# Stage 2 without a break between pairs of heads, and the first mixture's bias added block by block

## The chip, the cores and the metric

The kernel runs on one core of one Trainium2 chip, and the metric is device time in microseconds of one execution. PE is TensorE (its weight loads are PEld), DVE is VectorE, ACT is ScalarE, POOL is GpSimd, SP is SyncE, which here only issues transfers. Engines run their own instruction streams and wait for each other on semaphores.

## What is computed

A model of two layers over x of shape (4, 512, 128), in fp32: first a differential attention with 8 heads, beside a small attention over the batch with a mixture of 8 experts; then four layers of a selective scan with a second mixture. The change is in the first layer. What matters of the reference, cut:

```python
# attention: per head, two halves of q and k (8 columns each), gated by tanh of their difference
# first mixture, on the normed y of shape (2048, 128): each token goes to its argmax expert
idx = jnp.argmax(xf @ Wg.T, axis=-1)
for e in range(8):
    m = (idx == e)[:, None]
    h = jax.nn.relu(xf @ W1[e] + b1[e])
    out = out + m * (h @ W2[e] + b2[e])
# then layernorm of (y + out), a silu gate on the attention's output, and x + the product
```

## The kernel before

`build_stages` (line 48) writes six stages one after the other, each a block in which every engine has its own stream; a barrier of all engines stands between two stages. Tokens are 2048 = 16 tiles of 128. Stages 4 to 6 (line 1189 on: the second mixture, the scans, the output) are not touched.

**Stage 1** (lines 96 to 581) projects, makes q and k as sums of three bf16 parts, and does the small attention. SP stores the parts to `qk_dram` (line 181) and waits for them (line 182). The last work of the stage is the choice of each token's expert on DVE (`first_max`, lines 36 to 43, the last from 106.08 to 106.37 us), which gives `mask0`.

**Stage 2** (lines 588 to 980) has two jobs that share the engines.

The attention goes by steps. A head has 16 steps (4 batches b of 4 key blocks), a pair of heads 32; four steps with the same b are a unit, so a pair has 8 units. Per step PE makes one product into `bank_d` (`difference`, line 784) and two into `bank_l` (`scores`, lines 789 and 790); ACT makes the gate `gt` by tanh (line 877); DVE adds gate and scores into `tt` (lines 967 and 968); ACT takes exp into `ex` (line 883). In the next unit PE multiplies with the values into `bank_pv` (`weigh`, line 822, two halves), ACT copies that to `pvs` (`keep`, line 888), PE turns it back (`turn`, line 830), and DVE sums it into `ybig` (`settle`, line 957). Buffers are 2 banks of each kind and rings of 4 (`RING`). A loop over q, the pairs, is a hardware loop on every engine; at the end of each pass all of the pair's work is drained (lines 857 to 860, 912, 979).

The operands of `difference` and `scores` are the stacks `kst` and `qst` of two heads, [112, 2048] bf16, loaded by `load_head` (line 646) in 12 transfers per head of 32, 64 or 96 KB. At the start ACT loads its table (line 864, 1.28 us), the stacks are cleared (line 708 on POOL, 920 on DVE, two of 0.91 us) and the two first heads loaded, half of the first by ACT (line 870). Later heads are loaded by SP: the pair's next first head in the middle of the pair (line 687), its second at the end (line 696).

The mixture goes by blocks. DVE works out each token's row (lines 924 to 950, with three products on PE, lines 769 to 771, in between); then POOL scatters the 16 tiles into `yx_dram`, sorted by expert (line 735), in 24 blocks of 128 rows (`BLOCKS`; an expert starts a new block), after SP has written zeros there (line 671). Per block: SP loads its rows (`load_block`, line 674), PE turns them (`turn_block`, 796), ACT copies (`keep_in`, 892), PE makes the hidden layer (`hidden`, 802), DVE adds b1 and bounds at 0 (975), PE multiplies with W2 (`block_out`, 808), ACT copies (`keep_out`, 897), SP stores to `yo_dram` (691) and loads the rows two blocks on. POOL gathers a block's weights by indirect transfer (`gather_weights`, 721 to 727) when the block two before is done (`s_dn`). A pair works 6 blocks, in its units 2 to 7; units 0 and 1 have none. PE, ACT and DVE have a fixed order of all this by step, written out by hand (lines 837 to 856, 901 to 911, 961 to 978), and SP and POOL have one queue each:

```python
681 def turn(q, more):
682     for k in range(PER):
683         if k == 2 and more:
685             sp.wait_ge(s_L, step(q, 16))
687             load_head(sp, q * 2 + 2, 0)
689         sp.wait_ge(s_ek, blk(q, k + 1))
691         sp.dma_start(yo_dram[...], eo[k % 2][:, :])...
692         load_block(q * PER + (k + AHEAD), k % 2)
693     if more:
694         sp.wait_ge(s_L, step(q, 32))
696         load_head(sp, q * 2 + 3, 1)
```

**Stage 3** (lines 984 to 1183) norms the attention's output, and POOL gathers the expert outputs back (16 indirect transfers, line 1030), followed on POOL by the factors of two layernorms (`scale_and_offset`, lines 1033 to 1039). The bias b2 is added here: POOL clears `b2blk` (1026), SP fills its diagonal blocks by 16 transfers (1021), PE turns `mask0` (1088) and multiplies (1092, 16 products), and DVE adds the result (1130, 4 times).

## Time and profile before

| | us |
|---|---|
| median of 3 runs (1530.0 to 1530.98) | 1530.02 |
| the profiled execution | 1532.95 |
| its span, first to last instruction | 1530.7 |
| stage 1, to the first instruction of stage 2 | 107.9 |
| stage 2 | 107.9 to 421.7 |
| stage 3 | 421.7 to 475.96 |
| stages 4 to 6 | to 1530.7 |

Busy over the span: PE 82%, DVE 75%, ACT 68%, POOL 63%. A line of the timeline reads: start in us from the start of the span, length in us (a group's, where instructions follow each other, with the count at the end), engine, line, operation, what is written and read; in brackets the time for which the engine had been idle before it and who ended that. In the rows of stages, the clock is the mean granted clock of TensorE (1.00 is 2.4 GHz, 0.50 is 1.2 GHz), and the DMA share is that of the core's 16 DMA engines.

### The profile page before, as it was taken

What the parts mean: (1) busy time and instruction counts of PE and PEld (TensorE: products, weight loads), DVE (VectorE), ACT (ScalarE), POOL (GpSimd) and SP (SyncE); (2) the same over time, 40 slices, a digit from 0 to 9 for tenths busy, and PEclk for the clock granted to TensorE, in tenths of its full rate; (3) what the DMA queues carried; (4) which work ended last, traced back from release to release, by engine and by line L of the source; (5) the groups of instructions that cost most, each with busy time, mean ns of one, the idle gap of its engine ahead of it and who ended that gap; (6) DMA issues with size and microseconds to landing.
All of it is one profiled execution on the core that took longest, in us unless ns stands there. A gap on an engine that the chain in (4) does not pass through costs nothing. (4 is left out here: it accounts for less than half of the span.)

```text
span 1530.7 us, 21758 instructions
## 1 busy us (share of the span) xinstructions
PE 1255.4 (82%) x6427; PEld 620.1 (41%) x6427; DVE 1146.2 (75%) x1605; ACT 1045.8 (68%) x1804; POOL 965.2 (63%) x918
## 2 busy tenths in 40 slices
PE   6454689898836999977798998999899998999884
PEld 3341334343323547633343444444444444444331
DVE  7754468677786321238899999999999999999985
ACT  4323579788834122347588899888898889888871
POOL 5642311010185540058799898988998899989893
PEclk9775789899965999989899999999999999999988
DMA  2112232122214402330342344224341434234301
GB/s 59 42 46 98 89 97 84 65 89 72 86 30 160 132 21 66 114 84 24 83 104 71 77 95 97 71 71 108 85 98 55 99 87 106 59 73 95 93 8 55
DMA packets 84321, 120.47 MB, mean 79 GB/s; under 512 B 17410, under 2 KB 43256, under 8 KB 83848
## 3 DMA queue, kind: packets, MB, share of 16 engines
q1 hardware_dynamic: 77294, 100.60, 25.0%
q0 software_dynamic: 6816, 18.42, 4.0%
q8 instruction: 40, 0.66, 0.2%
q14 instruction: 49, 0.40, 0.1%
q10 hardware_dynamic: 122, 0.39, 0.1%
HBM read 96.15 MB, written 24.77 MB: 79 GB/s over the span
## 5 line engine op out<-in xcount | busy, mean ns | idle before, releaser
L2168 DVE TENSOR_TENSOR_SCAN hs<-decay,dbx 128x512 f32<-128x512 f32 x512 | 591.6, 1204 | 44.0 <-ACT decay L2050 20.4
L1746 POOL TENSOR_TENSOR hcm<-hs,Cc 128x1024 f32<-128x1024 f32 x192 | 452.9, 2367 | 24.6 <-DVE hs L2168 16.4
L2050 ACT ACTIVATE decay<-dtr,a_cur 128x512 f32<-128x512 f32 x512 | 350.7, 710 | 2.2 <-DVE hs L2168 1.9
L1870 PEld LDWEIGHTS dbx<-ident_sb,scaled 128*128 128x128 f32 x1536 | 178.5, 143 | 284.2 <-issue 126.7
L1870 PE MATMUL dbx<-ident_sb,scaled 128*128 128x128 f32 x1536 | 245.2, 284 | 52.8 <-POOL scaled L1729 27.3
L2028 ACT ACTIVATE scaled<-duT,BT 128x256 f32<-128x256 f32 x506 | 224.6, 496 | 27.4 <-PE dbx L1870 26.8
L1739 POOL TENSOR_TENSOR hck<-hs,Cc 128x512 f32<-128x512 f32 x128 | 163.3, 1276 | 54.5 <-DVE hs L2168 50.6
L1867 PE MATMUL dbx<-du,spread_sb 128*128 128x512 f32 x256 | 146.6, 656 | 12.5 <-DVE hs L2168 12.5
L883 ACT ACTIVATE ex<-tt 128x1024 f32<-128x1024 f32 x128 | 136.9, 1070 | 4.4 <-DVE tt L968 3.7
L1797 PE MATMUL slots<-XT,w_tap 128*128 128x512 f32 (+1 forms) x240 | 124.4, 606 | 3.8 <-PEq L1242 3.8
L1729 POOL TENSOR_SCALAR scaled<-duT,BT 128x256 f32<-128x256 f32 x256 | 118.3, 480 | 0.0
L967 DVE TENSOR_TENSOR tt<-bank_l,gt 128x512 f32<-128x512 f32 x128 | 87.5, 683 | 38.3 <-PE bank_l L790 34.6
L723 POOL CAST weight_rows<-w_row 128x1 uint32 (+1 forms) x26 | 4.8, 186 | 167.5 <-PE bank_e L808 167.5
L877 ACT ACTIVATE gt<-bank_d,dgh 128x512 f32<-128x512 f32 x128 | 89.1, 699 | 29.9 <-PE bank_d L784 29.9
L1887 PE MATMUL y_bank<-hcm,fold_sb 128*32 128x512 f32 x768 | 104.4, 616 | 4.2 <-POOL hcm L1746 4.2
L2158 DVE TENSOR_TENSOR dbx<-dbx,Bb 128x512 f32<-128x512 f32 x128 | 88.0, 688 | 23.5 <-PE dbx L1867 23.4
L968 DVE SCALAR_TENSOR_TENSOR tt<-bank_l,gt 128x512 f32<-128x512 f32 x128 | 87.0, 679 | 0.0
L1867 PEld LDWEIGHTS dbx<-du,spread_sb 128*128 128x128 f32 x256 | 43.9, 199 | 92.3 <-DVE hs L2168 46.8
L822 PE MATMUL bank_pv<-ex,v_head 128*32 128x512 f32 x512 | 74.8, 665 | 2.6 <-DVE ybig L957 2.6
L784 PE MATMUL bank_d<-q_stack,k_stack 112*128 112x512 bf16 x128 | 54.4, 430 | 13.4 <-DMA k_stack<-qk_parts 9.0
L1715 POOL MEMSET w_dt<- 41x256 f32 x1 | 0.3, 305 | 100.3 <-POOLq L1242 100.3
L1523 DVE TENSOR_TENSOR hid<-sil,u_bank 128x320 f32<-128x320 f32 x32 | 15.6, 487 | 62.3 <-ACT sil L1430 62.3
(331 smaller groups left out, 2026.5 us busy)
## 6 DMA issues: line engine op xcount, KB each, us to landing
dtr<-dt_turn SPq DMA_DIRECT2D x60, 512.0 KB, 7.7
Cc<-bc_turn SPq DMA_DIRECT2D x256, 64.0 KB, 2.1
dt_turn<-dt SPq DMA_DIRECT2D x15, 512.0 KB, 2.8
Bb<-bc_turn SPq DMA_DIRECT2D x64, 64.0 KB, 2.0
conv_row<-in_conv_row SPq DMA_DIRECT2D x4, 512.0 KB, 5.8
w_rg<-in_w_rg SPq DMA_DIRECT2D x8, 256.0 KB, 2.7
w_ru<-in_w_ru SPq DMA_DIRECT2D x8, 256.0 KB, 3.1
w_rd<-in_w_rd SPq DMA_DIRECT2D x8, 256.0 KB, 3.8
```

Source lines behind the costliest of these rows:

```text
L877: nc.scalar.activation(gt[:, st % RING, :], bank_d[st % 2][:, :], ACT.Tanh, scale=dgh[:, st // 16:st // 16 + 1]).then_inc(s_G, 1)
L883: nc.scalar.activation(ex[:, (st // 4) % 2, st % 4, :, :], tt[:, st % RING, :, :], ACT.Exp).then_inc(s_E, 1)
L1729: nc.gpsimd.tensor_scalar(scaled[:, (n + 1) % 2, kk, :, j, :], duT[:, n % 2, kk, :].rearrange("p (g c) -> p g c", c=32), BT[:, n % 2, kk, ...
L1739: nc.gpsimd.tensor_tensor(hck[:, g % KR, :], hs[:, p % HR, :], Cc[:, 3 + b % 2, :], ALU.mult).then_inc(s_hc, 1)
L1746: nc.gpsimd.tensor_tensor(hcm[:, (m - 1) % MR:m % MR + 1, :], hs[:, q % HR:p % HR + 1:p - q, :], Cc[:, k:k + 1, :].broadcast_to([P, 2, 512 ...
L1797: last = mm(dst[h][:, d:512], w_tap[:, 3 - d, P * h:P * h + P], XT[:, n % 4, 0:512 - d], start=(d == 0), stop=(d == 3))
L1867: mm(dbx[bank_of[p]][:, :], spread[:, g % 4, :], du[:, b % 2, g // 4, :], start=True, stop=True).then_inc(s_bx, 1)
L1870: last = nc.tensor.transpose(dbx[bank_of[p]][:, P * kk:P * kk + P], scaled[:, (b + k) % 2, kk, g, :, :].rearrange("p j c -> p (j c)"), ide ...
L1887: last = mm(y_bank[h][32 * q:32 * q + 32, :], fold[:, :], src, start=False, stop=((k, h) in ((DIRECT - 1, 0), (DIRECT, 1))), tile_position ...
L2028: nc.scalar.activation(scaled[:, (n + k) % 2, kk, :, j, :], duT[:, n % 2, kk, :].rearrange("p (g c) -> p g c", c=32), ACT.Copy, scale=BT[: ...
L2050: nc.scalar.activation(dec[:, p % DR, :], dtr[:, b % 2, g, :], ACT.Exp, scale=a_cur[:, 4 * g + k:4 * g + k + 1]).then_inc(s_dec, 1)
L2168: nc.vector.tensor_tensor_scan(hs[:, p % HR, :], dec[:, p % DR, :], dbx[bank_of[p]][:, :], 0.0, ALU.mult, ALU.add).then_inc(s_sc, 1)
```

## The change

1. The stacks of two heads live in the memory of `XT` and `GATE`, which stages 1 and 2 do not use otherwise. POOL clears the rows that no load writes, in stage 1, and SP loads heads 0 and 1 at the end of stage 1, behind the wait for the stored parts, and waits for them. ACT loads nothing any more.
2. The loop over pairs is one stream of steps: pair "-1" is written out, then a hardware loop of two, then the last pair. There is no drain between pairs; the last steps of a pair and the first of the next follow each other like any others.
3. `PER` is 8: the first pair has no blocks, each of the other three has eight, one in each unit. `BLOCKS` is 24 as before.
4. The working out of the rows (`route`) stands between the steps of the first pair: steps 0 to 4 and 8 to 13 on DVE, its products on PE after step 6. The scatter waits for the first ten steps' result, the gather of weights for the last.
5. SP loads the next heads in the first pair too, and at k = 4 (`PER // 2`) in place of k = 2.
6. b2 of a block's expert is gathered by POOL into `b2[i]` (an indirect transfer of 64 KB ahead of that of the weights, which now wait for `s_ek` in place of `s_dn`); `keep_out` is a DVE addition of `bank_e` and `b2`. What stage 3 did for b2 goes.

```diff
-            BLOCKS = 4 * (-(-(NT + NE - 1) // 4))
+            BLOCKS = 3 * (-(-(NT + NE - 1) // 3))
+            stacks = [tile[:, :, :].rearrange("p a b -> p (a b)").bitcast(bf16) for tile in (XT, GATE)]
+            qst = [stack[0:112, 0:T] for stack in stacks]
+            kst = [stack[0:112, T:2 * T] for stack in stacks]
...
                         sp.wait_ge(s_qkst, 16 * 6 * B)
+                        sp.wait_ge(s_z, 4)
+                        for i in range(2):
+                            load_head(sp, i, i, s_hl)
+                        sp.wait_ge(s_hl, 16 * 2 * LOADS)
...
+                        for stack in (qst[0], kst[0], qst[1], kst[1]):
+                            nc.gpsimd.memset(stack[32:64, :], 0.0).then_inc(s_z, 1)
...
-                        sp.wait_ge(s_z, 4)
-                        load_head(sp, 0, 0, (0,))
-                        load_head(sp, 1, 1)
                         sp.wait_ge(s_zz, 1)
...
+                        def next_head(q, i):
+                            sp.wait_ge(s_L, step(q, 16 * i + 16))
+                            sp.wait_ge(s_zz, 1)
+                            load_head(sp, q * 2 + (4 + i), i, s_ld[i])
+
+                        next_head(-1, 0)
                         sp.wait_ge(s_scat, 16 * NT)
                         for i in range(AHEAD):
                             load_block(i, i)
+                        next_head(-1, 1)
 
                         def turn(q, more):
                             for k in range(PER):
-                                if k == 2 and more:
-                                    sp.wait_ge(s_L, step(q, 16))
-                                    load_head(sp, q * 2 + 2, 0)
+                                if k == PER // 2 and more:
+                                    next_head(q, 0)
                                 sp.wait_ge(s_ek, blk(q, k + 1))
                                 sp.dma_start(yo_dram[bass.ds((q * PER + k) * P, P), :], eo[k % 2][:, :]).then_inc(s_es[k % 2], 16)
                                 load_block(q * PER + (k + AHEAD), k % 2)
                             if more:
-                                sp.wait_ge(s_L, step(q, 32))
-                                load_head(sp, q * 2 + 3, 1)
+                                next_head(q, 1)
-                        with sp.Fori(0, 3) as q:
+                        with sp.Fori(0, 2) as q:
                             turn(q, True)
-                        turn(3, False)
+                        turn(2, False)
...
                         def gather_weights(q, j, i, n):
-                            nc.gpsimd.tensor_copy(at_w[i][:, :], w_row[:, bass.ds(j, 1)]).then_inc(s_cur, 1)
+                            nc.gpsimd.tensor_copy(at_w[i][:, :], w_row[:, bass.ds(j, 1)])
+                            nc.gpsimd.tensor_copy(at_b[i][:, :], e_row[:, bass.ds(j, 1)]).then_inc(s_cur, 1)
                             pool.wait_ge(s_cur, blk(q, n + 1))
+                            nc.gpsimd.indirect_dma_start(b2[i][:, :], None, A["b2"], ...).then_inc(s_wl[i], 16)
                             nc.gpsimd.indirect_dma_start(weights[i][:, :], None, A["w_expert"], ...).then_inc(s_wl[i], 16)
...
                         pool.wait_ge(s_rows, 1)
...
+                        pool.wait_ge(s_rows, 2)
                         for i in range(AHEAD):
                             gather_weights(0, i, i, i)
+                        next_head(-1, 0)
+                        next_head(-1, 1)
...
-                                pool.wait_ge(s_dn, blk(q, k + 1))
+                                pool.wait_ge(s_ek, blk(q, k + 1))
                                 gather_weights(q, q * PER + (k + AHEAD), k % 2, k + AHEAD)
...
+                        def pair_of_heads(q, first=False, final=False):
                             for st in range(STEPS):
                                 u, mb = st // 4, st % 4
+                                if not (final and st >= STEPS - 2):
+                                    difference(q, st + 2, first)
+                                if not (final and st >= STEPS - 1):
+                                    scores(q, st + 1, first)
+                                if first and st == 6:
+                                    rank_tokens()
+                                if mb == 0 and not (first and u < 2):
                                     turn(q, u - 2)
+                                if mb == 0 and not first:
+                                    turn_block(q, u)
...
-                            turn(q, UNITS - 2)
-                            weigh(q, UNITS - 1, 0)
-                            weigh(q, UNITS - 1, 1)
-                            turn(q, UNITS - 1)
...
+                        def keep_out(q, k):
+                            dve.wait_ge(s_dn, blk(q, k + 1))
+                            dve.wait_ge(s_es[k % 2], loaded(q, k))
+                            TT(eo[k % 2][:, :], bank_e[:, 0, :], b2[k % 2][:, :], ALU.add).then_inc(s_ek, 1)
...
+                        def pair_of_heads(q, first=False):
+                            for st in range(STEPS):
+                                u, mb = st // 4, st % 4
+                                sums(q, st)
+                                if mb == 1 and not first:
+                                    relu(q, u)
+                                if mb == 3 and not first:
+                                    keep_out(q, u)
+                                if mb == 0 and not (first and u < 2):
+                                    settle(q, u - 2)
+                                if first:
+                                    route(st)
+
+                        pair_of_heads(-1, first=True)
+                        with dve.Fori(0, 2) as q:
+                            pair_of_heads(q)
+                        pair_of_heads(2)
+                        settle(2, UNITS - 2)
+                        settle(2, UNITS - 1)
...
-                        nc.gpsimd.memset(b2blk[:, :, :], 0.0).then_inc(s_z0, 1)
...
-                            link(TT(part(z, b), part(z, b), bank[4 + b][:, :, :], ALU.add))
```

## Rows read from the trace of the kernel before

**Rows 1.** Stages: us; busy (count) of PE, PEld, DVE, ACT, POOL; clock, DMA, GB/s
```profile
107.90:128.30 20.40, 3.14 (x11) 1.78 (x11) 10.23 (x26) 2.26 (x3) 7.23 (x12) 0.50 0.34 125
128.30:219.80 91.50, 62.37 (x346) 25.70 (x349) 49.19 (x95) 55.02 (x82) 26.11 (x34) 0.76 0.26 82
...
353.80:421.70 67.90, 59.28 (x374) 24.79 (x367) 49.88 (x97) 56.97 (x86) 7.71 (x15) 0.95 0.24 75
421.70:470.30 48.60, 14.11 (x89) 12.21 (x89) 43.24 (x104) 20.40 (x40) 39.58 (x47) 0.65 0.09 23
```

**Rows 2.** Timeline of PE: its three waits for a transfer
```profile
126.58 1.03 PE L784 MATMUL bank_d<-q_stack,k_stack 112*128 112x512 bf16 x2 [8.96 <-DMA k_stack<-qk_parts]
...
164.96 0.45 PE L796 MATMUL bank_e<-ident_sb,block_in 128*128 128x128 f32 x1 [23.39 <-DMA block_in<-block_rows]
...
201.55 0.47 PE L796 MATMUL bank_e<-ident_sb,block_in 128*128 128x128 f32 x1 [2.59 <-DMA block_in<-block_rows]
```

**Rows 3.** Timeline of PE: marks of one unit with a block
```profile
190.85 0.66 PE L830 MATMUL bank_pv<-ident_sb,pvs 128*128 128x128 f32 x4
...
192.20 1.16 PE L802 MATMUL bank_e<-block_inT,expert_weights 128*128 128x128 f32 x8
193.29 1.06 PE L822 MATMUL bank_pv<-ex,v_head 128*32 128x512 f32 x8
...
198.30 0.66 PE L830 MATMUL bank_pv<-ident_sb,pvs 128*128 128x128 f32 x4
```

**Rows 4.** Timeline of ACT: marks of one unit
```profile
209.80 0.60 ACT L888 ACTIVATE pvs<-bank_pv 128x512 f32<-128x512 f32 x1 [0.80 <-PE bank_pv L822]
210.29 0.27 ACT L897 ACTIVATE block_out<-bank_e 128x128 f32<-128x128 f32 x1
210.45 0.69 ACT L877 ACTIVATE gt<-bank_d,dgh 128x512 f32<-128x512 f32 x1
...
211.96 0.29 ACT L892 ACTIVATE block_inT<-bank_e 128x128 f32<-128x128 f32 x1
```

**Rows 5.** Timeline of DVE: first and last sums of pairs, last settle
```profile
128.31 0.69 DVE L967 TENSOR_TENSOR tt<-bank_l,gt 128x512 f32<-128x512 f32 x1 [6.94 <-PE bank_l L790]
...
224.10 0.68 DVE L968 SCALAR_TENSOR_TENSOR tt<-bank_l,gt 128x512 f32<-128x512 f32 x1
...
284.06 0.68 DVE L968 SCALAR_TENSOR_TENSOR tt<-bank_l,gt 128x512 f32<-128x512 f32 x1
...
291.81 0.68 DVE L968 SCALAR_TENSOR_TENSOR tt<-bank_l,gt 128x512 f32<-128x512 f32 x1
...
358.05 0.68 DVE L968 SCALAR_TENSOR_TENSOR tt<-bank_l,gt 128x512 f32<-128x512 f32 x1
...
412.58 0.68 DVE L968 SCALAR_TENSOR_TENSOR tt<-bank_l,gt 128x512 f32<-128x512 f32 x1
...
418.57 0.44 DVE L957 TENSOR_REDUCE ybig<-bank_pv 128x272 f32 x1 [3.50 <-PE bank_pv L830]
```

**Rows 6.** Timeline of SP's issues
```profile
84.43 1.44 SPq L181 DMA_DIRECT2D qk_parts<-part_k  x3
...
194.13 0.35 SPq L674 DMA_DIRECT2D block_in<-block_rows  x1
```

**Rows 7.** Transfer rate while one head loads; columns as in rows 1
```profile
221.00:232.30 11.30, 8.25 (x34) 2.08 (x34) 8.91 (x15) 9.80 (x14) 0.52 (x2) 0.79 0.20 72
```

**Rows 8.** Timeline of POOL: a wait in stage 1, scatter's end, stage 3
```profile
14.04 4.95 POOL L370 TENSOR_TENSOR ACC<-XN,b_mo 128x512 f32<-128x512 f32 x4 [11.89 <-DVE XN L280]
...
160.55 0.98 POOL L735 DMA_INDIRECT block_rows<-Y,row_u  x1 [0.31 <-issue]
...
421.68 1.80 POOL L1026 MEMSET b2blk<- 128x2048 f32 x1 [7.42 <-POOLq L645]
...
424.32 4.83 POOL L1030 DMA_INDIRECT ACC<-block_outs,row_u  x1 [0.80 <-POOL neghalf L1027]
```

**Rows 9.** Tile expert_weights: its gathers, issue to landing
```profile
DMA to landing us min/median/max: 4.4/4.7/8.1
```

More of the change, by code:

```diff
@@ new lines, in keep, with keep_in, pair_of_heads @@
+                        def keep(q, u):
+                            act.wait_ge(s_pvd, unit(q, u + 1))
+                            act.wait_ge(s_pvt, unit(q, u))
+                            nc.scalar.activation(pvs[:, :], bank_pv[:, :], ACT.Copy).then_inc(s_pvs, 1)
+                        def keep_in(q, k):
+                            act.wait_ge(s_xt, blk(q, k + 1))
+                            nc.scalar.activation(xbT[:, :], bank_e[:, 0, :], ACT.Copy).then_inc(s_xk, 1)
+                        def pair_of_heads(q, first=False, final=False):
+                            for st in range(STEPS):
+                                u, mb = st // 4, st % 4
+                                if not (final and st == STEPS - 1):
+                                    gate(q, st + 1)
+                                if not (first and st == 0):
+                                    exps(q, st - 1)
+                                if mb == 3 and not (first and u == 0):
+                                    keep(q, u - 1)
+                                if mb == 0 and not first:
+                                    keep_in(q, u)
@@ L915, in _ @@
+                        gate(-1, 0)
+                        pair_of_heads(-1, first=True)
+                        with act.Fori(0, 2) as q:
+                            pair_of_heads(q)
+                        pair_of_heads(2, final=True)
+                        exps(2, STEPS - 1)
+                        keep(2, UNITS - 1)
                     @block.vector
```

356 lines of the change are left out of this document (158 added, 198 removed).

## The prediction

> **What bounds the kernel now.** The profiled execution took 1532.95 us, its span is 1530.7 us, and the median of the three runs is 1530.02 us. I work out a difference against the profiled execution and take it off the median, since the 2.9 us between them is nothing that the change touches. A change of 0.2% is 3.1 us, about what a measurement of this kernel can tell from no change.
>
> I read the stages first. Stages 4 to 6 begin at 475.96 us and are untouched, so only three stretches count [rows 1]: the opening of stage 2 (107.9 to 128.3 us, DVE busy 10.2 of 20.4), its four pairs of heads (128.3 to 421.7), and stage 3 (421.7 to about 470). The first pair takes 91.5 us and the last 67.9 [rows 1], for the same work. The timeline of PE says why [rows 2]: PE waits 8.96 us for the stacks of q and k before the first product, 23.39 us for the first block's rows in pair 0 (scattered only by then), and 2.59 us for a block's rows at 201.55 us.
>
> Inside a pair two rates matter. A unit of four steps with an expert block is PE's: from one L830 to the next is 7.45 us [rows 3], back to back. The block's `hidden` takes 1.09 us of it (192.20 to 193.29), `block_out` as much, so a unit without a block is 5.27 us of PE at 2.4 GHz. On ACT a step is 1.51 us and the copy of pvs adds 0.49 [rows 4]: 4 x 1.51 + 0.49 = 6.5 us. So a unit without a block is ACT's. At the end of a pair all drains: the last L968 of pair 1 is at 284.06, the first of pair 2 at 291.81, 7.75 us where a step is 1.9 [rows 5].
>
> **The change, part by part.**
>
> *Stacks loaded in stage 1.* SP's last store of stage 1 ends its issue at 85.87 [rows 6]; two more for landing, then 24 loads of 1.57 MB together. One head (786 KB) moves at 72 GB/s [rows 7], so 11 us; two are 22, plus 2 until the first bytes. 88 + 24 gives 112, and as these loads share with nothing better than in that row I take 114 (bounds 112 and 118, the latter at 55 GB/s). Stage 1 else ends at 106.4, so the waiting SP now holds the barrier: 114 + 1.5 = 115.5 for the first instructions of stage 2 (1.5 is the distance 106.4 to 107.9 now). The four memsets of 32 partitions on POOL lie in its wait of 11.89 us that ends at 14.04 [rows 8], and cost nothing. In stage 2 ACT still loads its table (1.28) and runs one gate; the first L967 stands at 117.6, where it is 128.31 now [rows 5]. That is 10.7 us gained; next late is SP, no longer PE.
>
> The row shows 72 GB/s at a DMA share of 0.20 [rows 7]. The Trainium skill ("DMA: Bandwidth & Descriptors", Specifications) gives about 358 GB/s as a core's limit to HBM. By that figure 1.57 MB would take an estimated 4.4 us, stage 1 would end with its own work and the kernel at 1483. The row decides.
>
> *Pair 0 without blocks, with the routing between its steps.* The 26 us at the first block go altogether (23.39 on PE [rows 2]): scatter and gathers now lie under pair 0. Eight ACT units of 6.5 us are 52. PE runs at 1.2 GHz when the stage opens (clock 0.50 [rows 1]); I add 3 us for that. The routing's 8.4 us of DVE (10.23 less the two memsets of stacks, 0.91 each [rows 1]) come on steps in which DVE has 1.2 us of work out of 1.5 to 1.9: I take 5 of the 8.4 as seen. Pair 0 is 60 us; bounds 53 and 71.
>
> Is the first block there in time? Rows are known after step 10, some 23 us into the pair (141); 16 scatters at 1.29 (0.98 + 0.31 [rows 8]) and landing give 164; the loads stand behind head 2's, 168; weights by 170. Pair 1 starts at 178: 8 us to spare.
>
> *Pairs 1 to 3, each with eight blocks and no drain.* Pairs 1 and 2 take 8 x 7.45 = 59.6 each. The last takes what it takes now from its first sums to the last settle, 419.0 - 357.4 = 61.6 [rows 5], plus 3 because its first two units become 14.9; now they are 54.5 less 23 steps of 1.86, 11.7 [rows 3, 5]. The b2 gather on POOL, 24 more, and a cast each, are hidden: POOL is busy 7.7 of 67.9 us [rows 1]. The gather of weights is now asked for after `keep_out` and stands behind that of b2: some 2.6 us later. A block's weights are wanted 14.9 us less about 4.3 after that point, 10.6; needed are 1.3 of casts, 1.3 for b2 and 4.7 for the landing, 7.3, and 10.7 where the landing takes 8.1 [rows 9]. So they just hold. `keep_out` moves from ACT to DVE, which has room (49.9 of 67.9 [rows 1]); it no longer waits behind the copy of pvs, 0.5 us [rows 4].
>
> *Head loads on SP, in the middle of pairs and now between them too.* This is what gives back. Today the load of block 4's rows is issued at 194.13 [rows 6], behind a head's twelve loads, and lands 7.4 us later, at 201.5: PE's wait of 2.59 [rows 2], and a slow clock after it. Its price is the difference of pair 1 and pair 3 from first to last L968: 59.96 - 54.53 = 5.4 us [rows 5]. It falls three times now. With blocks in every unit the same collision comes after the load at k = 4 (pairs 1 and 2) and after the load at a pair's end (pairs 2 and 3), four times; at pair 1's start SP is free three us earlier and I count 0.5. Less the 0.5 of the earlier `keep_out`, 4 x 4.9 + 0.5 = 20.1 us (bounds 0 and 28).
>
> *Stage 3.* The memset of b2blk (1.80), the 16 loads, 16 products and four additions go. The chain there is POOL's, busy 39.6 of 48.6 us [rows 1]: after that memset the gathers, from 424.32 [rows 8], then the factors. It starts 1.8 us earlier. The additions lie beside POOL's work. 1.8 us (bounds 1 and 5.5: the first gather's 4.83 may turn to 1.0).
>
> **Sum.** 117.6 + 60 + 119.2 + 64.6 + 20.1 = 381.5 for the last settle, 419.0 now: 37.5 less. With 1.8 of stage 3, 39.3. 1530.0 - 39.3 = 1490.7; I say 1491 (the profiled execution would be 1493.7).
>
> **Rivals.**
> *Half clock in pair 0.* PE with gaps may keep 1.2 GHz. In the stretch [rows 7] it was 0.79 with PE busy 8.25 of 11.3 us. Then a unit without block is PE's, near twice 5.27 less overlap, 8.9 us: 71 for 60, 1502. Against it: at 5.27 of 6.5 us PE is busier than there. The skill ("TensorE: Matmul & The Clock Gate", Part 1) ties the clock to PE's recent activity, in which the trace agrees.
> *The collisions vanish.* If the earlier stores and a faster drain bring the rows in before PE asks, the 20 us stay: 1471. For: it is late by 2.59 only. Against: nothing shortens SP's queue.
> *The opening or the first blocks are late.* Head loads at 55 GB/s, or pair 1 waiting some 5 us for weights: 1500.
> *Slower than before: POOL becomes the bound.* The first gather of stage 3 took 4.83 us instead of 1.0 [rows 8], beside a DVE operation. If both gathers of a block did, a block would cost POOL 2 x 5.13 + 1.3 = 11.6 us for a unit of 7.45: 24 x 4.1 = 99 us, 1590. It decides from 3.6 us a gather on (24 x 1.6 eats the 39). Against: weights land after 4.7 [rows 9] beside the same DVE sums (the scatters at 0.98 [rows 8] ran while DVE stood). The skill ("SBUF — State Buffer", who interferes with whom) says that DVE's two-port operations keep GpSimd from writing descriptors, which speaks for it; but the sums read PSUM, and stay as they are.
> *It doesn't do what it says*: the loads in stage 1 only move the wait ahead of the barrier and pair 0 is stretched by the routing to what the drain was: within 3 us of 1530; the 23.39 us speak against it.
>
> **Chances.** Sum 0.60, half clock 0.12, collisions gone 0.14, late opening 0.09, POOL 0.03, no effect 0.02. Faster 0.95, same 0.02, slower 0.03. The range takes in half clock and late opening with 4 us each above, and half of the gain of vanished collisions with a short opening below: 1474 to 1506.
>
> **What would show it.** Right: stage 2's first sums near 117.6, PE without a wait for block_in in pair 0; from pair to pair of L968 60 us and then about 65; PE's waits for block_in, some 2.6 us each, at units 2 and 6 of the pairs. Wrong: POOL's indirect transfers over 1.3 us in the loop; DVE or PE waiting for expert_weights or expert_bias; clock 0.50 through pair 0; SP's issue of block loads far from the head loads with PE still waiting.

## The result, and the profile after

| | kernel before | changed kernel |
|---|---|---|
| median of 4 runs, us | 1530.01 (1527.91 to 1530.98) | 1494.47 (1492.36 to 1497.9) |
| ratio, 95% interval | 1 | 0.9772 (0.9751 to 0.9793) |
| span of the profiled execution, us | 1530.7 | 1496.1 |
| first sums of stage 2 | 128.31 | 116.24 |
| pair 0 | 95.19 | 56.13 |
| pair 1, pair 2 | 67.70, 66.24 | 68.68, 68.23 |
| last pair, first to last sums | 54.55 | 65.20 |
| end of the last settle | 419.01 | 381.29 |
| VectorE's first instruction of stage 3 | 421.72 | 388.78 |
| first instruction of stage 4 | 475.96 | 442.10 |

A pair is counted here from its first sums (L943/L944, L967/L968 before) to those of the next. The change makes the kernel 2.3% faster, 35.5 us. 1491 was forecast, in a range of 1474 to 1506.

The stages of the changed kernel, in the columns of [rows 1]: pairs 0 to 3 and stage 3.

```profile
116.20:172.40 56.20, 48.04 (x239) 12.58 (x239) 47.51 (x96) 51.35 (x69) 21.96 (x27) 0.81 0.27 88
172.40:241.10 68.70, 63.21 (x393) 29.79 (x392) 53.30 (x113) 57.31 (x83) 17.48 (x34) 0.93 0.36 98
241.10:309.30 68.20, 62.32 (x393) 29.36 (x392) 53.27 (x113) 56.09 (x81) 19.57 (x36) 0.95 0.41 108
309.30:381.30 72.00, 63.16 (x412) 29.90 (x411) 53.50 (x114) 56.77 (x81) 21.06 (x36) 0.95 0.39 98
388.70:442.10 53.40, 13.70 (x64) 11.05 (x64) 40.51 (x100) 25.03 (x49) 40.17 (x50) 0.56 0.08 20
```

Where [rows 1] show pair 0 with PE busy 62.37 of 91.5 us, it is busy 48.04 of 56.2 now, at a mean clock of 0.81. The three pairs with eight blocks have PE busy 62 to 63 of 68 to 72 us; what is left is waiting. Between 381.3 and 388.7 there is a hole.

The waits of PE in pairs 1 to 3, from the view of the waits (us in total, times, longest):

```profile
PE bank_e L809 <- DMA block_in<-block_rows: 14.3, 4, 6.2
PE bank_e L815 <- DMA expert_weights<-in_w_expert,weight_rows: 2.3, 4, 1.1
```

The same waits in the timeline of PE; the fourth is the longest:

```profile
224.87 0.48 PE L809 MATMUL bank_e<-ident_sb,block_in 128*128 128x128 f32 x1 [3.24 <-DMA block_in<-block_rows]
...
259.77 0.33 PE L809 MATMUL bank_e<-ident_sb,block_in 128*128 128x128 f32 x1 [2.37 <-DMA block_in<-block_rows]
...
294.00 0.33 PE L809 MATMUL bank_e<-ident_sb,block_in 128*128 128x128 f32 x1 [2.49 <-DMA block_in<-block_rows]
...
331.57 0.47 PE L809 MATMUL bank_e<-ident_sb,block_in 128*128 128x128 f32 x1 [6.23 <-DMA block_in<-block_rows]
```

They answer to the 2.59 at 201.55 of [rows 2]; the 23.39 of that group is gone. SP's issues ahead of the last of them show why:

```profile
309.20 0.33 SPq L679 DMA_DIRECT2D block_in<-block_rows  x1
309.87 2.02 SPq L102 DMA_DIRECT2D GATE<-qk_parts  x3
312.09 2.24 SPq L104 DMA_DIRECT2D GATE<-qk_parts  x3
314.55 1.99 SPq L102 DMA_DIRECT2D GATE<-qk_parts  x3
316.73 2.08 SPq L104 DMA_DIRECT2D GATE<-qk_parts  x3
319.08 0.38 SPq L698 DMA_DIRECT2D block_outs<-block_out  x1
319.51 0.42 SPq L679 DMA_DIRECT2D block_in<-block_rows  x1
```

The block's load at 319.51 stands behind twelve loads of a head whose bytes are still on their way, and PE has its rows at 331.57, 12 us later.

The end of stage 2 on POOL, the two fetches for a block that doesn't exist, and stage 3's start; below it VectorE's first instruction of stage 3:

```profile
376.03 0.18 POOL L719 CAST weight_rows<-w_row 128x1 uint32<-128x1 f32 x1 [3.83 <-DVE block_out L965]
...
377.20 1.02 POOL L723 DMA_INDIRECT expert_bias<-in_b,bias_rows  x1 [0.87 <-POOL bias_rows L720]
378.52 1.00 POOL L725 DMA_INDIRECT expert_weights<-in_w_expert,weight_rows  x1 [0.30 <-issue]
388.74 0.10 POOL L1061 MEMSET neghalf<- 128x4 f32 x1 [9.21 <-POOLq L667]
...
390.95 5.24 POOL L1064 DMA_INDIRECT ACC<-block_outs,row_u  x1 [0.30 <-issue]
```
```profile
388.78 1.75 DVE L1172 RECIPROCAL rs<-ybig 128x256 f32<-128x256 f32 x1 [7.49 <-PEq L667]
...
390.89 4.43 DVE L1175 TENSOR_TENSOR ybig<-ybig,rs 128x4096 f32<-128x4096 f32 x1
```

POOL idles 9.21 us behind the last gather, and VectorE 7.49 behind the last settle, where before stage 3 began 2.67 behind it (419.01 to 421.68 [rows 5, 8]). The wait is named after PE's queue, which had long been done.

### The profile page after: what moved, and what is told of

It is laid out like the page before. It is cut to its first block and busy times, and to the rows that moved or that the text cites. A ratio compares the mean times of both kernels' runs of the same rounds, so it can differ in the third digit from the quotient of the medians.

```text
span 1496.1 us, 21378 instructions
## 1 busy us (share of the span) xinstructions
PE 1243.2 (83%) x6394; PEld 613.1 (41%) x6394; DVE 1142.0 (76%) x1624; ACT 1042.1 (70%) x1779; POOL 996.9 (67%) x971
## 5 line engine op out<-in xcount | busy, mean ns | idle before, releaser
L943 DVE TENSOR_TENSOR tt<-bank_l,gt 128x512 f32<-128x512 f32 x128 | 87.7, 685 | 37.7 <-PE bank_l L794 35.2
L944 DVE SCALAR_TENSOR_TENSOR tt<-bank_l,gt 128x512 f32<-128x512 f32 x128 | 87.2, 681 | 0.0
L1546 DVE TENSOR_TENSOR hid<-sil,u_bank 128x320 f32<-128x320 f32 x32 | 15.6, 488 | 62.3 <-ACT sil L1453 62.3
L1479 DVE TENSOR_TENSOR hid<-sil,u_bank 128x512 f32<-128x512 f32 x32 | 22.0, 687 | 49.7 <-ACT sil L1435 49.4
```

## The experiments

Twelve kernels: the changed one again (e5) and eleven variants of it. One plain fact is needed for the first four, each of which has a single run: beside them the kernel before took 1560.69 us, each one's stages 4 to 6 took some 30 us more than in the changed kernel (1084 to 1088 for 1054), and one unit of pair 0 took 19 to 23 us (its engines wait there mostly for nothing that the profile names). The chip's number on record is the same for them as for e5 to e8, so whether it was another chip or another time isn't shown, and the cause stays open. These four are read by units and marks of pairs 1 to 3 and not by their total. Beside the other eight the kernel before takes 1526 to 1529.

### e1: no head is loaded behind the first two

```diff
-                            sp.wait_ge(s_L, step(q, 16 * i + 16))
                             sp.wait_ge(s_zz, 1)
-                            load_head(sp, q * 2 + (4 + i), i, s_ld[i])
...
-                            if st % 16 == 0 and not (first and st < STEPS):
-                                pe.wait_ge(s_ld[i], ...)
```

> Leaves out: heads 2 to 7 are never loaded in stage 2 (72 transfers), so pairs 1 to 3 compute with the stacks of heads 0 and 1. Theory (a block's rows stand behind a head's twelve loads): PE's waits for block_in, 14.3 us in four places, go to 0, the landing of block rows falls from 8.0 to 4 us, every unit of pairs 1 to 3 takes 7.34 us, pairs 1 and 2 take 58.8 and 58.8 us in place of 68.7 and 68.2, the kernel about 1467. Rival (the b2 gather ahead of the weights is what makes blocks late, loads or not): waits for block_in go, but waits for expert_weights stay or grow, pairs over 63 us, kernel over 1480.

Measured: 1514.91 us. All units of pairs 1 to 3 take 7.30 to 7.43 us but the first of pair 1, 9.64. The view of PE's waits from 183 to 368 us has nothing of a block or of weights in it:

```profile
PE bank_pv L838 <- ACT pvs L902: 2.2, 3, 0.7
PE bank_d L784 <- ACT gt L891: 0.6, 1, 0.6
PE bank_pv L830 <- DVE ybig L947: 0.5, 1, 0.5
```

So the head loads make all the stalls, those for the weights too, and without them a unit is 7.34: below the 7.45 that I took from [rows 3]. The 9.64 is not a stall for a transfer. In the changed kernel that unit takes 10.22 us and has the eight products of L815 at 1.93, where they take 1.16 later, and the granted clock is 0.50 for 3.4 us of it. Two stretches of the changed kernel with that clock, the first in this unit and the second behind the longest wait for a block, and then the same unit in e11, in the columns of [rows 1]:

```profile
175.60:179.00 3.40, 3.40 (x16) 1.64 (x15) 2.07 (x6) 2.72 (x4) 0.00 (x0) 0.50 0.26 88
329.20:336.00 6.80, 4.43 (x20) 2.29 (x20) 0.94 (x4) 3.32 (x5) 0.00 (x0) 0.50 0.10 39
173.00:181.70 8.70, 7.52 (x50) 3.60 (x50) 6.63 (x14) 8.38 (x14) 0.53 (x3) 1.00 0.06 22
```

But the clock is only part of it: with a clock of 1.00 throughout (e3, e4, e6, e11, e12) the unit still takes 8.53 to 8.61, 1.2 above 7.34 (1.1 above the 7.46 of e6). In e11 PE waits three times for ScalarE in it, 0.58, 0.72 and 0.38 us. So of the 2.9 us in the changed kernel 1.7 go with the clock (10.22 against 8.54), and 1.2 do not. In the twelve the unit takes 7.70 to 10.22 us.

### e2: each head's loads in pieces, between the blocks

```diff
-                                if k == PER // 2 and more:
-                                    next_head(q, 0)
                                 load_block(q * PER + (k + AHEAD), k % 2)
+                                if k in (0, 1):
+                                    load_head(sp, q * 2 + 3, 1, s_ld[1], ((1,), (2, 3))[k])
+                                if k in (3, 4, 5) and more:
+                                    next_head(q, 0, ((0,), (1,), (2, 3))[k - 3])
                             if more:
-                                next_head(q, 1)
+                                next_head(q, 1, (0,))
```

> The same transfers, but each head's twelve in four groups of three, put behind the block loads of successive blocks (1, 1 and 2 groups). Theory (queue): most of what the kernel without head loads gains comes without leaving anything out: PE's waits for block_in under 3 us in total in place of 14.3, pairs 1 and 2 at 59 to 62 us, kernel 1467 to 1474. Rival (the bandwidth that head loads take, wherever they stand, is what costs): pairs stay at 66 or more, the waits only spread over more blocks, kernel within 5 us of 1494.

Measured: 1534.9 us. The waits for block_in are gone, and the longest unit of pairs 1 to 3 is 11.92 where e3, of the same group, has four of 11.8 to 12.0. What came in their place is PE's wait for weights, 6.9 us in 4, and 0.9 for a stack. Units 4 and 8 are the long ones now, and those waits stand in them, where weights are gathered while the last piece of a head (six loads at once) is on its way. That the size of this piece is the reason isn't shown: e8 has finer pieces and waits for weights still. Over the 22 units behind that first one the sum above 7.34 is 11.5 us for e2 and 20.2 for e3.

### e3: nothing is fetched for the two blocks behind the last

```diff
-                                load_block(q * PER + (k + AHEAD), k % 2)
+                                if more or k < PER - AHEAD:
+                                    load_block(q * PER + (k + AHEAD), k % 2)
...
+                                if not more and k >= PER - AHEAD:
+                                    continue
                                 pool.wait_ge(s_ek, blk(q, k + 1))
                                 gather_weights(q, q * PER + (k + AHEAD), k % 2, k + AHEAD)
```

> The last pair no longer gathers weights and b2, nor loads rows, for two blocks beyond the last. Theory: stage 3 begins 7.4 us after the last settle because POOL's last gathers (issued until 379.5, landed at 382.8) and what POOL needs to close behind them are late; it is 2.7 us before. Without them stage 3 begins some 2.7 us after the last settle again: 4.8 us gained, kernel 1489 to 1490. Rival (the barrier is late because of code loading or SP's stores, not POOL): under 1 us.

Measured: 1532.12 us, the last settle at 388.90 and VectorE's first instruction of stage 3 at 389.23, 0.33 behind it. That is the whole hole, and more than it: the 2.7 us of the kernel before go as well. The edit takes two loads of SP away too, but these weren't what held the stage: in the changed kernel the last of them had landed 2.0 us after its issue at 376.38, before the last settle.

### e4: the weights are asked for when the block's last product is done, ahead of the bias

```diff
-                                pool.wait_ge(s_ek, blk(q, k + 1))
+                                pool.wait_ge(s_dn, blk(q, k + 1))
                                 gather_weights(...)
...
+                            nc.gpsimd.indirect_dma_start(weights[i][:, :], ...).then_inc(s_wl[i], 16)
+                            if n >= AHEAD:
+                                pool.wait_ge(s_ek, blk(q, n - AHEAD + 1))
                             nc.gpsimd.indirect_dma_start(b2[i][:, :], ...).then_inc(s_wl[i], 16)
```

> The weights are gathered as before the change, when block_out is done and ahead of b2; b2 follows when keep_out is done. Theory: PE's four waits for expert_weights (2.3 us) and the long units before the collisions (8.46, 7.92) go, 3 to 4 us in pairs 1 to 3; the waits for block_in stay within 2 us of 14.3; kernel 1490 to 1491. Rival (the gather of weights is what holds the block's rows up): the waits for block_in fall by over a third.

Measured: 1539.07 us. PE no longer waits for weights, but for block_in 13.1 us in 4: the wait that came last was the block's anyway, the sum above 7.34 is 21.3 us against e3's 20.2, and the 3 to 4 us that the theory gave did not come. Nor did the rival's third of the waits. Stage 3 begins 5.66 us behind the last settle (394.57 to 400.23) in place of 7.45, with the last gather issued 1.3 us earlier against it (4.1 us before its end, 2.8 in the changed kernel).

### e5: the changed kernel again

> The changed kernel itself, unaltered, as the base of this group. The runs so far of its variants were on a chip on which the kernel before took 1560 us, with one unit of pair 0 of 19 to 23 us in place of 5.7. Theory (that stall belongs to the chip or to the moment, not to the change): the ratio to the kernel before is 0.975 to 0.979 again, first sums at 116.2, pair 0 56, last settle 381, stage 3's first instruction 388.7, so some 35 us less than the kernel before. Rival (the stall belongs to the changed kernel, whose pair 0 now does more at once): pair 0 takes 68 to 75 here too and the ratio is 0.982 to 0.988.

Measured: 1493.9 us, ratio 0.9765 (0.9715 to 0.9815). Pair 0 takes 56.07 us, the last settle ends at 378.10, and stage 3 begins 7.58 behind it. The theory holds. The last settle is 3.2 us earlier, and one unit makes more than that: the third of the last pair takes 11.81 for 15.77, as PE waits 3.7 us there in place of 6.23 and then has the clock of 0.50 for 3.4 us in place of 6.8. So two executions of one kernel differ by some 3 us in the stalls of stage 2.

### e6: the bias as before the change

```diff
-                            nc.gpsimd.indirect_dma_start(b2[i][:, :], None, A["b2"], ...)
-                            TT(eo[k % 2][:, :], bank_e[:, 0, :], b2[k % 2][:, :], ALU.add).then_inc(s_ek, 1)
+                            nc.scalar.activation(eo[k % 2][:, :], bank_e[:, 0, :], ACT.Copy).then_inc(s_ek, 1)
...
+                            last = nc.tensor.matmul(bank[4 + t // 4][:, t % 4, :], maskT[:, :], b2blk[:, t, :], start=True, stop=True)
```

> Only the bias is put back: no gather of it and no cast for it by block, keep_out a copy on ScalarE, the weights asked for when the block's last product is done, and the bias in stage 3 by the masked product of the kernel before. Stage 2 stays overlapped as in the change. Theory (the bias by block costs more than it gives: its gather shares the transfer engines with the head loads, it stands ahead of the weights on GpSimd, and it lengthens the dead gathers behind the last block): waits for the weights (2.3 us in the changed kernel) go, the last settle is 1 to 3 us earlier (378 to 380), stage 3 begins 5 to 6 after it in place of 7.4, stage 3 is 0.9 longer: 2 to 5 us faster than the changed kernel. Rival 1 (it is worth what it takes out of stage 3 and costs nothing in stage 2): 1 us slower. Rival 2 (the copy on ScalarE, which lengthens units to the 7.45 that the kernel before shows in place of 7.34): 24 units times 0.11, 2.6 us, plus 0.9: 3 to 4 us slower.

Measured: 1485.92 us, 8.0 less than e5, more than the 2 to 5 that I expected (ratio 0.9715, 0.9665 to 0.9765; the profiled executions differ by 8.2). By marks: the last settle 373.12 for 378.10, stage 3's first instruction 2.94 behind it for 7.58, stage 3 54.2 for 53.8. So the bias by block gains 0.4 us in stage 3, and in stage 2 a shorter unit, 7.34 for 7.46: with ScalarE's copy a unit is 0.12 longer, 2.8 us in 23. The copy (0.27 us) stands ahead of that of the block's rows, which in e6 is done at 233.63, and `hidden` starts at 233.68, 0.44 behind the product ahead of it, where in e11 it is 0.32. The bias by block gives back more. PE's waits in e6, for a block and nothing for weights:

```profile
PE bank_e L803 <- DMA block_in<-block_rows: 8.7, 4, 2.3
```

The sum above the undisturbed unit, without the first, is 15.1 us here and 22.2 in e5: 7.1 more with the bias by block, of which 3.1 are waits for a block and 2.2 waits for weights. The packets show what goes with it: from its first to its last packet a head takes some 13.6 us (58 KB/us) in e6 and 15.6 to 16.7 (47 to 50) in e5, which has one more gather for each block on its way. It is not their number alone: e4 has as many, behind those of the weights, three of its four heads take 13.6 to 14.3 us, and it waits for blocks for 13.1 us all the same. What part the number and the place of the gathers have isn't shown. And the tail takes 4.6. So the bias by block costs 7.1 + 4.6 - 2.8 - 0.4 = 8.5 us. The rest of the 9.2 by which stage 4 begins earlier has other sources: pair 1's first unit has 1.8 less above the undisturbed one in e6 (its clock stays at 1.00), opening and pair 0 together are 1.1 longer. Rival 2's term, the copy, was there, and did not decide.

### e7: all routing ahead of pair 0

```diff
+                        for st in range(14):
+                            route(st)
                         pair_of_heads(-1, first=True)
...
-                                if first:
-                                    route(st)
```

> Only the overlap of the routing with pair 0 is taken back: VectorE routes all 14 parts and ranks the tokens ahead of pair 0's first difference, as in the kernel before; the run from pair to pair stays. Theory (the routing is work that VectorE must do once, and moving it into pair 0 hides part of it where VectorE has room): first sums at 127 to 129 in place of 116.2, pair 0 51 to 54 in place of 56.1, so last settle 7 to 10 us later than in the changed kernel and the total 7 to 10 us slower. Rival (VectorE sets pair 0's pace, so routing costs the same wherever it stands): pair 0 44 to 46, no difference beyond 1.5 us. Second rival (scatter and first blocks come earlier when the routing is first, and relieve the first units of pair 1): up to 3 us of the loss comes back in pair 1 unit 0.

Measured: 1496.74 us, 2.8 more than e5; by the marks 1.3 (stage 4 begins at 440.75 for 439.44), the rest lies in stages 4 to 6, which are the same code. The 7 to 10 us of the theory did not come; what came lies hardly beyond the noise (1495.5 to 1499.1 for 1492.6 to 1496.1). VectorE's routing ends and the first sums follow:

```profile
124.26 0.24 DVE L999 TENSOR_SCALAR w_row<-w_row,lane_sb 128x26 f32<-128x26 f32 x1
124.75 0.69 DVE L942 TENSOR_TENSOR tt<-bank_l,gt 128x512 f32<-128x512 f32 x1 [0.25 <-DVE w_row L999]
```

The opening is 8.65 us longer (116.10 to 124.75), pair 0 4.53 shorter (51.54 for 56.07): between the steps the routing costs a little over half of what it costs ahead of them. Of the 4.1 us that are left 2.5 come back in pair 1's first unit, 7.70 for 10.22. That is the second rival's size but not its reason, since no transfer was late there in either: L815's eight products take 1.16 us in e7 (at 178.43) and 1.97 in e5, whose granted clock from 172.2 to 182.4 is 0.83. In e7 the 3.4 us at a clock of 0.50 lie ahead of it, from 170.2 to 173.6, in pair 0's last unit (7.60 us for 6.70).

### e8: finer pieces, and no dead tail

```diff
+                                if k in (0, 1):
+                                    load_head(sp, q * 2 + 3, 1, s_ld[1], ((1, 2), (3,))[k])
+                                if k in (3, 4, 5) and more:
+                                    next_head(q, 0, ((0,), (1, 2), (3,))[k - 3])
```

The edit of e3 is in it too.

> Two edits together: the 12 loads of each head's stack go out in pieces of 3, 6 and 3, one behind each block's load (stack 0 behind blocks 3, 4, 5, stack 1 behind the pair's end and blocks 0, 1), so that no block waits behind a whole stack, and the loads and gathers for the two blocks that don't exist are left out. Theory (the 6 units that are longer than 7.34 wait for a block queued behind a stack, and stage 3 starts 4.8 us late for the dead gathers): the waits for block_in (14.3 us) go but for 1 or 2, stage 3 begins 2 to 4 us after the last settle in place of 7.4: 10 to 17 us faster than the changed kernel. Rival (the queue's rate of 42 to 70 KB/us sets how long a stack takes whatever the order, so the wait moves from the block to the stack, at units 3 and 7, as in the coarser spread where pieces of 3, 3 and 6 left waits of 1 to 5 us there): only the tail's 4 to 5 us are gained.

Measured: 1474.07 us, ratio 0.9633 (0.9585 to 0.9681), 19.8 less than e5: more than expected. The last settle comes 13.4 earlier (364.67), stage 3 begins 0.33 behind it (7.3 gained). PE waits for no block; what is late next is the weights:

```profile
PE bank_e L823 <- DMA expert_weights<-in_w_expert,weight_rows: 6.1, 6, 2.9
```

### e9: the short tail alone

The edit of e3.

> Only the loads and gathers for the two blocks behind the last real one are left out, as in e3_no_dead_tail, which ran on the chip of 1560 us and there showed the last sums settled at 388.9 and no more than some 2.5 us up to stage 3's first instruction. Theory (stage 3 waits for GpSimd to close behind these gathers; 0.3 us remained in e8_spread_short_tail in place of 7.5): stage 3's VectorE starts 0.3 to 0.8 us after the last settle, so 6.5 to 7.5 us less than the changed kernel, 1486 to 1488 where that takes 1494; units as in the changed kernel, but for the last pair's third, which may lose 0 to 3 us of its wait. Rival (the gap belongs to all engines meeting at the end of the stage, whatever GpSimd does): the gap stays at 2.7, as in the kernel before, and 4 to 5 us are gained.

Measured: 1487.86 us, ratio 0.9746 (0.9731 to 0.9761). Last settle at 377.70 (e5: 378.10), and

```profile
377.99 0.10 POOL L1064 MEMSET neghalf<- 128x4 f32 x1 [16.73 <-POOLq L667]
...
378.03 1.75 DVE L1175 RECIPROCAL rs<-ybig 128x256 f32<-128x256 f32 x1 [0.33 <-PEq L667]
```

Where POOL has been idle for 16.73 us it opens stage 3 at once, and VectorE waits 0.33. The rival, a gap that belongs to the meeting of the engines, falls.

### e10: e8 with the bias as before

> The edits of e8_spread_short_tail and of e6_b2_as_before together: stacks in pieces, nothing fetched behind the last block, the bias in stage 3 by the masked product. Theory (the bias's gather costs by its share of the transfer engines and by its place ahead of the weights, and both costs are in what e8 still shows: 6.1 us of waits for the weights, stacks at 42 to 46 KB/us): the waits for the weights go, units are 7.46 in place of 7.34 (24 times 0.12, 2.9 us back), stage 3 and what follows 1 to 1.5 longer: 1 to 3 us less than e8, ratio to the kernel before 0.961 to 0.963. Rival (e6's 8 us were its tail, 4.6, and the head loads' speed, both of which e8 already has): e8's time plus 2.9 plus 1.4, 3 to 4 us more than e8, ratio 0.9655.

Measured: 1468.54 us, ratio 0.9622 (0.9609 to 0.9635). Units are 7.45 or 7.46 but for the first of pair 1 (9.64) and the two where pairs meet (7.37 and 7.55), with no wait for any transfer; stage 4 begins at 411.30 (e8: 418.31). The ratio moved less than the marks, 0.0011 from e8's with e8's interval of 0.005 to each side; the marks say 7.0 us less.

### e11: e8 with a wait of the bias's own

```diff
+                s_wb = [sem(f"bias_gathered{i}") for i in range(2)]
...
-                                pool.wait_ge(s_ek, blk(q, k + 1))
+                                pool.wait_ge(s_dn, blk(q, k + 1))
+                                pool.wait_ge(s_wb[k % 2], loaded(q, k))
...
+                            dve.wait_ge(s_wb[k % 2], loaded(q, k))
                             TT(eo[k % 2][:, :], bank_e[:, 0, :], b2[k % 2][:, :], ALU.add).then_inc(s_ek, 1)
```

> The edits of e8_spread_short_tail, and the bias stays by block, but with a wait of its own: the weights are asked for as soon as the block's last product is done, the bias behind them once its buffer is free, and only VectorE's addition waits for it. Theory (e8's 6.1 us of waits for the weights are the 1.3 us of the bias's gather ahead of them, the 1 us between the product and the addition, and a wait that counts both): weights are asked for 2.3 us earlier and waited for 0 to 2 us in all, units at 7.34: 3 to 5 us less than e8, ratio to the kernel before 0.960 to 0.9615. Rival (the weights are late because the transfer engines carry a stack then, not because they are asked for late): 0 to 1.5 us less, the longest wait still above 2.

Measured: 1467.04 us, ratio 0.9611 (0.9592 to 0.9629). PE's waits from 172 to 355 us, all of them of 0.4 us and more:

```profile
PE bank_pv L855 <- ACT pvs L919: 2.2, 3, 0.7
PE bank_d L801 <- ACT gt L908: 0.6, 1, 0.6
PE bank_pv L847 <- DVE ybig L964: 0.5, 1, 0.5
PE bank_e L828 <- ACT block_inT L923: 0.4, 1, 0.4
```

Every unit of pairs 1 to 3 takes 7.25 to 7.43 us but the first, 8.53. Stage 4 begins at 408.82, 9.5 us before e8's (1.7 of it in that first unit) and 2.5 before e10's: rid of the waits, the bias by block is worth its shorter unit (2.8 us) and its 0.7 in stage 3, and opening, pair 0 and the unit behind it together take 1.0 of that back. The edit asks for the weights earlier and parts the two waits; which of the two did it isn't told apart, but the rival falls: the longer runs of a head's loads (9 or 12) come at 41 to 45 KB/us here, much as in e8 (36 to 47), and nothing waits. The medians of e10 and e11 can't be told apart.

### e12: a head's rows together in DRAM

```diff
-            qk_dram = nc.dram_tensor("qk_parts", [2, 3, P, T], bf16).ap()
+            qk_dram = nc.dram_tensor("qk_parts", [2, 3 * P, T], bf16).ap()
...
-                             qk_dram[1, part:part + 1, rows, :].broadcast_to([k, 8, T])).then_inc(done, 16)
+                             qk_dram[1, bass.ds(h * 48 + (24 * s + 8 * part), 8 * k), :]).then_inc(done, 16)
```

> e11_spread_tail_own_wait with another layout of the parts of q and k in DRAM: a head's rows of all three parts stand together (24 rows), those of k in the order 2, 1, 0, so that each of a head's 12 loads is one run of 24, 16 or 8 rows and none repeats a part. Bytes, packets (192 of 4 KB for a head) and loads are the same. In the traces so far a packet of 4 KB takes 0.159 us, and while heads load the queue's packets fill 17% of the 16 transfer engines, so 2.7 are at work. Theory (a load is spread over as many engines as its outermost count allows, 3, 2 and 8 for the three shapes now, so a head takes 4 x (8 + 8 + 1) x 0.159 = 10.8 us, the 11 that are seen): with 12, 16 and 8 engines it is 4 x (2 + 1 + 1) x 0.159 = 2.5 us, and the issue on the sync queue (16 us for two heads, from 87.1) is what is left: last bytes at 105 in place of 111.3, stage 2's first instruction at 106.5 to 108.5 in place of 113.3, first sums 5 to 6.5 us earlier, and the total 5 to 7 us less than e11, ratio to the kernel before 0.957 to 0.958. Rival (rows of 4 KB to few partitions are slow wherever they come from): 70 KB/us again, no difference beyond 1 us. Second rival (stage 1's own work ends late): first sums at most 3 us earlier.

Measured: 1461.53 us, ratio 0.9566 (0.9545 to 0.9588), 5.5 less than e11. The two heads' packets start within 10.7 us (147 KB/us) where the changed kernel takes 22.4, and no longer hold the stage: SP's issues in e12, the last loads and the first of stage 2:

```profile
96.10 1.41 SPq L103 DMA_DIRECT2D GATE<-qk_parts  x3
97.56 1.04 SPq L106 DMA_DIRECT2D GATE<-qk_parts  x3
109.05 0.36 SPq L674 DMA_DIRECT2D tile_starts_sb<-in_tile_starts  x1
```

The 24 issues take 9.1 us where they took 15.9 (87.13 to 103.03), so even SP's queue is quicker. What is late next is stage 1's own work on VectorE, as the second rival has it:

```profile
105.56 0.29 DVE L38 COPY ss<-s_bank 128x128 f32<-128x128 f32 x1 [3.76 <-PE s_bank L557]
...
107.18 0.29 DVE L43 TENSOR_TENSOR mask<-ss,amax 128x128 f32<-128x128 f32 x1
```

First sums at 112.00, where the changed kernel has 116.24 and e11 117.54. By the marks less is left of these 5.5 us than the medians say: pair 0 takes 57.56 for 55.69, and stage 4 begins 3.6 earlier than in e11 (405.18 for 408.82).

## Why the prediction was right, and where its steps were not

The forecast, 1491, is 3.5 us below what was measured, and what it foretold of pair 0 and of the collisions took place. But the sum is so good because its errors cancel. In the profiled execution:

| term | forecast | measured | off by |
|---|---|---|---|
| first sums | 117.6 | 116.24 | -1.4 |
| pair 0 | 60 | 56.13 | -3.9 |
| 24 units with a block and the drain | 183.8 | 180.8 | -3.0 |
| pair 1's first unit above the others (1.7 by the lower clock) | 0 | 2.9 | +2.9 |
| collisions of block and head loads | 20.1 | 25.2 | +5.1 |
| last settle | 381.5 | 381.29 | -0.2 |
| gap to stage 3 | 2.7 | 7.5 | +4.8 |
| gain in stage 3 | 1.8 | 0.9 | +0.9 |

- *Opening.* Right: SP's head loads hold the barrier (stage 2's first instruction at 113.28), at 70 KB/us by the packets where [rows 7] gave 72. I weighed the Trainium skill's figure for a core's path to HBM ("DMA: Bandwidth & Descriptors", Specifications) against that row and let the row decide. e12 shows what the row was made of. It is no limit of the memory: with the same bytes in 24, 16 and 8 rows to a load the rate is 147. A packet of 4 KB takes 0.159 us in the median. The same page of the Trainium skill ("Why a DMA increments its semaphore by 16 and not by 1") has the rule: a transfer is spread over the largest number of engines up to 16 that divides the slowest dimension of both patterns. By it 3, 2 and 8 engines for the old shapes make an estimated 10.8 us a head, where 11.2 was seen, so in time the runs agree for these; for the new ones they show only that the rate at least doubles, since SP's issue takes 9.1 of the 10.7 us and a packet takes 0.253 us there. The engine of a packet stands in no row here.
- *Pair 0.* I took 52 for ScalarE's pace, 3 for the clock and 5 for the routing. The routing was right: 4.5 us (e7 against e5). The 3 for the clock was wrong: with the routing elsewhere the pair takes 51.5, so nothing is left for it there. I had none one pair later, where 1.7 was due: pair 1's first unit takes 10.22 us with 3.4 at a clock of 0.50 and 8.54 with none. Another 1.2 of that unit, with PE behind ScalarE, I had not either. The rival of half clock through the pair did not come; the mean was 0.81, and there was no wait for a block in it.
- *Units.* 7.34, not 7.45: the 0.11 goes with ScalarE's copy of the block's output, which the change takes from the loop. I had noted that `keep_out` leaves ScalarE and gave it a value only in the collisions. e6, with the copy back, has 7.46.
- *Collisions.* The mechanism was right, four waits for block_in, where they were foretold and none at pair 1's third unit; e1 shows that nothing else stalls. The size was not: 4.9 each came from one collision without any gather of a bias [rows 5]. e6 has 15.1 us of them in 4, and the bias by block makes it 22.2 (e5) to 25.2. Of the 25.2 PE's waits are 14.3 + 2.3; the other 8.6 go with a clock of 0.50 in four stretches around them, 20.4 us together, where e10, e11 and e12 without such waits have 1.00 from 176 to 355. What I wrote of the 24 gathers, that they are hidden because POOL has room, looked at the engine that issues them and not at what they do to other transfers. The margin of the weights was as narrow as I had it (landing 7.2 to 8.6 us while a head loads) and cost 2.3 us.
- *The gap to stage 3: the step that I missed.* I carried 2.7 us over without asking what it was made of. It is POOL's last gather, of a block that isn't there, and its end: [rows 8] have POOL idle 7.42 us behind it. The change asks for that gather 3 us later against the last settle (2.77 before its end where it was 5.76), since it now waits for the addition and stands behind the bias's, and POOL then takes 9.21 in place of 7.42 us: 3.0 + 1.8 = 4.8. Nor was it the landing alone: that gather lands 4.1 us after its issue (4.4 before), at 382.6, and from there POOL takes 6.1 us to stage 3, where it took 4.0 before. e3, e8 and e9 take the gathers away, and the gap is 0.3 in each.
- *Stage 3.* The memset's 1.80 is off the front as forecast, but the slow gather only moved from the first to the second (4.83 to 5.24 us), and 0.9 is what came out.
- *POOL as the bound*, the rival on the other side: the gathers in the loop took 1.00 to 1.02 us, all 48. It was priced soundly and did not come.

So of the change's parts the first five together are worth 43.3 us (e6 against the kernel before), and the sixth, the bias by block, costs 8 to 8.5 as it was built (e5 against e6). With the waits mended the latter gains 2.5 by the marks (e11 against e10), which the medians do not confirm. The best version, e12, is 33 us faster than the changed kernel by the medians of two groups of runs, 4.3% below the kernel before.

## What to carry to other kernels

When a transfer is added to a loop, ask not only which engine issues it but which transfers are on their way with it, and which wait on a shared semaphore it delays. Ask of every gap at the end of a stage what is made of it: a prefetch of nothing behind the last iteration costs nothing until it is the last thing that ends. And a low transfer rate is a question about the shape of the transfer before it is a price.

## What was not expected of the hardware

- POOL is slow to leave a stage behind indirect gathers: 7.42 us after the last one's end with a gather of weights alone (7.45 in e6), 9.21 to 9.56 with a bias's ahead of it (the changed kernel, e1, e2, e5, e7; 8.77 with the bias's behind, e4). Counted from the last gather's landing it is the same each time: 4.0 us with the weights alone (before, e6), 6.1 with the bias (the changed kernel, e4, e5, e7). What these 4.0 and 6.1 us are made of is not named in the trace.
- A gather takes 4.8 to 5.2 us to issue beside VectorE's L1175, whose two inputs both lie in SBUF (390.89 to 395.32, the gather 390.95 to 396.19), in every kernel here, and 1.00 to 1.44 otherwise. The Trainium skill ("SBUF — State Buffer", Who interferes with whom) infers that such an operation leaves the writing of descriptors alone. This one held the issue; but the gather also reads its row numbers from SBUF, and beside L1181, with two inputs in SBUF too, one takes 1.00 (396.50). Which of these it hangs on isn't shown.
- A load's rate depends on how its rows are grouped: 70 and 147 KB/us for the same 1.57 MB, and the issue on SP 0.65 and 0.37 us in the mean of 24.
- In one group of runs the kernel that takes 1526 to 1530 us otherwise took 1560.69, and one unit of pair 0 was held up by 13 to 17 us in each of four kernels. Why wasn't tried.
